# A transformer block on eight cores: LayerNorm row sums moved to VectorE, and the softmax row sums of flash attention issued ahead of the P·V matmuls

## The reference, cut to what matters

```
xn  = layernorm(x)
y   = attention_block(xn)      # layernorm, QKV, rope, causal softmax(QK^T/8)V, Wo, residual,
                               # layernorm, GELU MLP, residual
z   = moe(xn) + 0.1*shared(xn) # 8 experts, top-2 weights, SiLU, inner size 4096
out = x + y + z
```

## Time and profile before

| what | value |
|---|---|
| median of 3 runs | 10069.1 us |
| profiled execution | 10075.5 us, span 10073.9 us on core 1 |
| spans of the 8 cores | 10039.6 to 10073.9 us |
| PE busy | 7646.4 us (76%), mean granted clock 0.860 |
| DVE, ACT busy | 3351.0 us (33%), 2940.1 us (29%) |
| statistics and Q | from 0 to about 530 us |
| chunks with attention | from about 530 to 4630 us |
| the rest (Wo, MLP, experts) | from there to the end |

### The profile page before, as it was taken

The page is one execution under the profiler, slowest core; times in us unless marked ns, Lnnn a source line. Parts: engine busy times, 40 slices in busy tenths (PEclk is TensorE's granted clock), DMA queues, the critical chain, the costliest instruction groups (busy, mean ns, idle before and its releaser), DMA issues.

```text
span 10073.9 us, 105868 instructions; the slowest of 8 cores (10039.6 to 10073.9 us)
## 1 busy us (share of the span) xinstructions
PE 7646.4 (76%) x33092; PEld 2919.7 (29%) x33092; DVE 3351.0 (33%) x5932; ACT 2940.1 (29%) x3541; POOL 486.5 (5%) x860
## 2 busy tenths in 40 slices
PE   2256776666666666665489699999999999999998
PEld 0011111111111111112234243434343434444444
DVE  3233333333334334444433332323232322222212
ACT  4544553444443333322011121111111111111110
POOL 0000000000000000000011000000000000000000
PEclk7578887888877777676699899999999999999999
DMA  4421001111101211121221211121212122211111
GB/s 119 123 39 27 18 9 27 27 27 23 22 9 37 34 33 29 27 48 21 38 38 30 34 34 34 34 38 30 42 26 42 26 42 38 38 34 34 34 34 51
DMA packets 218705, 365.43 MB, mean 36 GB/s; under 512 B 20008, under 2 KB 115624, under 8 KB 218176
## 3 DMA queue, kind: packets, MB, share of 16 engines
q0 software_dynamic: 182848, 251.76, 15.8%
q1 hardware_dynamic: 35328, 106.89, 3.5%
HBM read 601.89 MB, written 8.39 MB: 61 GB/s over the span
## 4 chain that ended last, share of the span: by engine, by line
PE 71%; DVE 15%; ACT 6%; issue 5%; DMA 3%; DVEq 1%; POOL 0%; ACTq 0%; SPq 0%; POOLq 0%
PE pst L62 57%; PE ps_l L62 8%; PE pav L62 5%; DVE acc L62 5%; DVE tmp L62 2%; DVE st L62 1%; ACT xsta L62 1%; DVE ntok L62 1%; DVE qg L62 1%; DMA wp1b<-MW 1%; DVE nf L62 1%; ACT pt_a L62 1%; ACT pt_b L62 1%; ACT vbuf L62 1%; DVE kbuf L62 1%
## 5 line engine op out<-in xcount | busy, mean ns | idle before, releaser
L62 ACT ACTIVATE actb<-pst,biasf 128x512 bf16<-128x512 f32 x1280 | 879.7, 687 | 3414.7 <-PE pst L62 3414.6
L62 PE MATMUL pst<-actb,wp2a 128*128 128x512 bf16 x5632 | 1412.8, 379 | 71.8 <-DVE actb L62 57.4
L62 DVE TENSOR_TENSOR acc<-acc,pst 128x512 f32<-128x512 f32 x1312 | 902.9, 688 | 1609.8 <-PE pst L62 1604.3
L62 PE MATMUL pst<-actb,wp2b 128*128 128x512 bf16 x4608 | 1182.6, 379 | 0.0
L62 DVE TENSOR_TENSOR actb<-actb,cwb 128x512 bf16<-128x512 bf16 x1024 | 435.7, 425 | 1555.3 <-ACT actb L62 1555.3
L62 DVE SCALAR_TENSOR_TENSOR acc<-acc,stats,pav 64x512 f32<-64x512 f32 x640 | 477.4, 746 | 1072.4 <-PE ps_l L62 953.7
L62 PEld LDWEIGHTS pst<-actb,wp2a 128*128 128x128 bf16 x5632 | 522.3, 98 | 743.7 <-issue 162.5
L62 PE MATMUL pst<-qg,kbuf 64*128 64x512 bf16 x2560 | 566.0, 444 | 64.9 <-ACT pt_a L62 16.7
L62 PEld LDWEIGHTS pst<-actb,wp2b 128*128 128x128 bf16 x4608 | 450.9, 98 | 543.7
L62 ACT ACTIVATE pt_b<-pst,stats 128x1024 bf16<-128x1024 f32 x427 | 475.8, 1114 | 425.0 <-PE pst L62 402.6
L62 ACT ACTIVATE pt_c<-pst,stats 128x1024 bf16<-128x1024 f32 x426 | 474.7, 1114 | 403.3 <-PE pst L62 380.3
(11 more groups left out here) (185 smaller groups left out, 7910.2 us busy)
## 6 DMA issues: line engine op xcount, KB each, us to landing
wstr<-Wqkv POOLq DMA_DIRECT2D x144, 512.0 KB, 5.8
xsta<-x_pref SPq DMA_DIRECT2D x128, 512.0 KB, 4.4
wp1a<-MW POOLq DMA_DIRECT2D x128, 256.0 KB, 5.5
wp1b<-MW POOLq DMA_DIRECT2D x128, 256.0 KB, 8.5
wp2a<-MW POOLq DMA_DIRECT2D x128, 256.0 KB, 5.5
wp2b<-MW POOLq DMA_DIRECT2D x128, 256.0 KB, 8.7
xsta<-x_own SPq DMA_DIRECT2D x48, 512.0 KB, 4.7
wstr<-Wo POOLq DMA_DIRECT2D x16, 512.0 KB, 6.7
```

What stands on the lines that cost most here:

```text
L62: ins = getattr(E, meth)(*args, **kw)
```

## The change

There are two edits. In `stat_tile` the sum of a tile comes from a `reduce_sum` on VectorE; ScalarE's Identity pass goes away, and its Square, which overwrites the tile, now waits for VectorE. SP's loads of a slot wait for both. In `emit_avl` the two row-sum matmuls go ahead of the two value matmuls. The wait for `fl_acc` stays in front of the values, and so stands behind the row sums now. The semaphore that ends a group is raised by the second value matmul.

```diff
             xt = xsta[:, slot * D:(slot + 1) * D]
+            b.wait("v", sxs[slot], xl)
+            b.red("reduce_sum", lns[:, t:t + 1], xt, sem=sv)
+            lncons[slot][0] = sv.n
             b.wait("s", sxs[slot], xl)
-            b.act(xt, xt, AF.Identity, accum=lns[:, t:t + 1])
+            b.wait("s", sv)
             b.act(xt, xt, AF.Square, accum=lns[:, 80 + t:81 + t], sem=ss)
...
                     if first_l:
                         b.wait("t", sv, fl_lev[0])
+                    b.mm(ps_l[0:16, 0:512],
+                         oh16[:, 16 * (2 * hp_):16 * (2 * hp_) + 16],
+                         ptb[:, 0:512], start=first_l, stop=False)
+                    b.mm(ps_l[0:16, 0:512],
+                         oh16[:, 16 * (2 * hp_ + 1):16 * (2 * hp_ + 1) + 16],
+                         ptb[:, 512:1024], start=False, stop=last)
+                    first_l = False
                     if kt_ == 0:
                         b.wait("t", sv, max(fl_acc[0], fl_acc[1],
...
                          ptb[:, 0:512], tp=(0, 0),
                          start=(kt_ == 0), stop=(kt_ == 3))
-                    b.mm(pav[64:128, 512:1024],
...
-                    b.mm(ps_l[0:16, 0:512],
...
-                    av = b.mm(ps_l[0:16, 0:512],
...
-                    first_l = False
+                    av = b.mm(pav[64:128, 512:1024],
+                              vbuf[:, kt_ * D + hp_ * 128 + 64:
+                                   kt_ * D + hp_ * 128 + 128],
+                              ptb[:, 512:1024], tp=(0, 64),
+                              start=(kt_ == 0), stop=(kt_ == 3), sem=st)
                     fl_avl[pt3] = av
```

More of the change, by code:

```diff
@@ L623, in emit_avl @@
                          start=(kt_ == 0), stop=(kt_ == 3))
-                    b.mm(pav[64:128, 512:1024],
[L625 to L628, removed]
-                    b.mm(ps_l[0:16, 0:512],
-                         oh16[:, 16 * (2 * hp_):16 * (2 * hp_) + 16],
-                         ptb[:, 0:512], start=first_l, stop=False)
-                    av = b.mm(ps_l[0:16, 0:512],
[L633 to L636, removed]
-                    first_l = False
+                    av = b.mm(pav[64:128, 512:1024],
[3 more added lines that the diff above has]
+                              start=(kt_ == 0), stop=(kt_ == 3), sem=st)
                     fl_avl[pt3] = av
```

## The result

The changed kernel ran in 9780.9 to 9807.9 us where nothing disturbed it (four executions), against 10068.5 and 10069.1 us for the kernel before. The ratio is 0.9725, with a 95% interval of 0.9691 to 0.9759: 2.75% faster, about 277 us, where 323 us and 9746 us were forecast.

What follows compares the result with a forecast made beforehand. TensorE, busy 76% of the span, bounds the kernel, its value matmuls waiting for VectorE's addition. 89 (unmasked wait) + 53 (unmasked clock) + 168 (masked steps) + 13 (statistics) = 323 us off 10069, 9746 us; range 9630 to 9890.

Steps and rivals of the forecast that it cites:

- The wait itself: Attention: row-sum matmuls hide in TensorE's wait for the accumulator addition; 89 us unmasked, 106 masked, together 195 us.
- the rival of the untouched clock: Whole kernel: clock stays as it is, only hidden matmuls and statistics count; 208 us saved, 9861 us; chance 0.20.
- The clock in unmasked steps: Unmasked attention steps: less TensorE idle time removes 1.5 clock drops a step; 53 us, ends none or 67.
- The clock in masked steps: Masked attention steps: period falls from 10.06 to 8.56 us, hidden matmuls included; 168 us, ends 106 and 293.
- Statistics: Tile sums before attention: moving them from ScalarE to VectorE saves 13 us; ends 35 saved or 10 lost.
- SP's wait: Statistics: SP's rope load waits for all 16 sums, holding `x_own` loads behind it; leaves 1 us a batch in three batches.
- some 3 us sooner: Statistics, first batch: it waits for VectorE until 28.5 us and ends some 3 us sooner.
- a slot's turn: Statistics: load, sum, Square and gaps take 7.7 us for four tiles in place of 9.92.
- A whole recovery: Attention: the clock recovers whole in unmasked and masked steps; 462 us saved, 9607 us; chance 0.10.
- Dear neighbours: Attention matmuls: new neighbours cost the score pairing, 340 us lost against 208 gained, 10201 us; chance 0.05.
- an addition slow down while TensorE writes `ps_l`: VectorE's addition, reading `pav` meanwhile, takes 0.5 us more in 280 waits; 140 us back, 9886 us; chance 0.04.
- the clock terms: Attention: savings from more full clock in unmasked and masked steps; the skill page was read as speaking against them.

Runs made afterwards that it cites:

- e4: Kernel before, old order, plus two unused row-sum-shaped matmuls ahead of the waiting value matmuls in seven head pairs a step; 9913.8 and 9915.4 us.
- e2: Kernel before with only the statistics edit (tile sum on VectorE), attention in its old order; fastest time 10051.5 us.
- e16: Kernel before with only the new order (row sums ahead of values), statistics as before, run again for an undisturbed profile; 9790.2 and 9797.8 us.
- e1: The changed kernel run once more with no edit, for a profile; fastest time 9790.0 us.
- e17: Kernel before, old order, with unused matmuls ahead of the waiting values, two in unmasked steps and six in masked ones; 9806.9 us.
- e5: Changed kernel plus six unused matmuls between row sums and waiting values in masked steps; fastest 9777.4 us with one die disturbed, undisturbed die 9622 to 9655.

## Why the prediction was right or wrong

The kernel came out near 9792 us, 46 us above the forecast and inside its range. The mechanism was right; one term of the sum was too large.

*The wait itself.* Right. 1.07 us is left, periods of 5.89 against 5.88. The waits view gives 174 us less in all, 88 in unmasked steps (89 forecast) and 86, or 0.77 a wait, in masked ones. The 195 us that the section on the wait adds up, and the rival of the untouched clock with it, priced the masked waits at the lower clock throughout, 0.95 us; the sum of the forecast itself has 0.73 for them, 82 us, which is close.

*The clock in unmasked steps.* Right in mechanism and size: 53 us by letting 1.5 drops a step go. All went. Summed over the seven periods of the 24 steps, e4, where nothing is hidden, is 51 us shorter than before, and the changed kernel 140, which is the 88 of the wait and 52 of the clock. Another 9 us lie between the last addition of one step and the first of the next, which the forecast didn't look at; so it is 149 us and not 142.

*The clock in masked steps.* Right in mechanism and in regime (0.76 forecast, 0.76 and 0.78 in the windows), wrong in size: 168 us forecast, 122 measured. The step that failed is the mean masked period of the kernel before, "(13 x 10.24 + 3 x 9.29) / 16 = 10.06 us". The 10.24 was one period from the middle of a step, and I took it for all seven; the last of a step is some 2 us shorter, and the first 0.8. VectorE's additions in the very step that it was taken from show both:

```profile
1306.30 1.60 DVE L62 SCALAR_TENSOR_TENSOR acc<-acc,stats,pav 64x512 f32<-64x512 f32 x2
...
1315.71 1.59 DVE L62 SCALAR_TENSOR_TENSOR acc<-acc,stats,pav 64x512 f32<-64x512 f32 x2
...
1366.94 1.60 DVE L62 SCALAR_TENSOR_TENSOR acc<-acc,stats,pav 64x512 f32<-64x512 f32 x2
...
1375.02 1.60 DVE L62 SCALAR_TENSOR_TENSOR acc<-acc,stats,pav 64x512 f32<-64x512 f32 x2 [1.75 <-PE ps_l L62]
```

The first period is 9.41 us, the last 8.08, and the mean of the seven 9.82. The 9.29, from which the 8.56 was worked out, was a mean over seven. Over seven, and over all 16 masked steps, the kernel before has 9.73, not 10.06. With that, the same working gives 9.73 - 8.56 = 1.17, x 112 = 131 us, next to the measured 1.09 x 112 = 122. Of the 46 us by which the forecast was too high, this is 37. Put by cause, of the 168 us the forecast had 86 for the clock (168 - 82), and the runs show 36 (122 - 86).

*Statistics.* 13 us forecast; at the first score, 12 measured in e2 and 10 in the changed kernel as means over the cores, and 5 on the pair of cores in the table. The price of a sum (1.2 against 1.22) was right, and so was SP's wait in kind. By batches, from the mean ends of the four normalisations behind each one, before and in e2: the first ends 1.7 us later (79.9 and 81.6 us), where "some 3 us sooner" was forecast; the next three gain 1.8, 3.7 and 1.8 us, where 1 each was; the last gains 6.0, where 7 was. The first batch is what failed: VectorE's first instruction on the finished sums, which began at 61.03 us before, begins at 62.43 in the changed kernel and at 62.69 in e2 (cores of the table). As e2's second batch shows, the sums stand up to 2 us for their loads, so that a slot's turn was longer than the 7.7 us of the working. At the end of the whole kernel nothing of this is seen (e16).

*The rivals.* An untouched clock (9861 us) is out by the windows of e1 and by e4. A whole recovery (9607) came true in unmasked steps alone. Dear neighbours (10201) did not come: 0.32 and 0.34 us. Nor did an addition slow down while TensorE writes `ps_l`: it takes 1.60 us as before. What the page TensorE: Matmul & The Clock Gate of the Trainium skill says in "Loop structure matters more than you think", that VectorE's copy doesn't break the warmth, agrees with e17 if it is taken by the word: the copy is as before there and the clock is up. But in the loop that the page shows the next matmuls follow immediately, and here they waited, so the page does not speak against the clock terms as the prediction had it. It is the idle time that the wait for the copy leaves on TensorE that costs; with the clock untouched the gain would have been 208 us, and it was 277.

The sum against the traces, for the two cores of the table: waits 171 us forecast and 174 measured, clock 139 (53 + 86) and 87 (51 + 36), statistics 13 and 5; 9 us between unmasked steps, 5 after attention and 3 or 4 elsewhere were in no term. That makes the 284 us between the spans. Why a masked step of the changed kernel swings between 8.5 and 9.6 us a period and doesn't settle, as it does in e5 with the idle time filled, was not tried.

## What to carry to other kernels

When an engine must wait for a single buffer, put whatever is ready on its queue ahead of the waiting instruction, and look at what is left for more: row sums, then the next scores. On TensorE such a wait can count twice, as it did here: once as lost time and once for the clock that it costs the matmuls around it. The test is cheap, since matmuls with unused results in the gap show the second part alone. And take all numbers that are subtracted from one another from the same set of periods: a middle period less a mean over seven made up 37 of the 46 us of error here.

## What was not expected of the hardware

That useless work would pay so well. In the kernel before, 560 unused matmuls, two a wait, took some 160 us off 10074 (e4), and 1008 of them, two a wait in unmasked steps and six in masked ones, took 264 off (e17: 9809.8 us), nearly as much as the change itself (284). In masked steps idle stretches of 3.12 us in periods of 10.24 us went with a clock of 0.68, stretches of 1.46 us in periods of 7.97 with 1.00 between the additions of a step (0.95 with the stretch ahead of them); in unmasked steps 1.60 went with 0.94 and 1.07 with 1.00.
